# Cross-attention with image keys on one core: the statistics' transposes in another PSUM bank, and the result rows finished by ScalarE and GpSimd

## What is computed

```python
q = _split_heads(hidden_states @ w_q, HEADS)
k = _split_heads(text @ w_k, HEADS)
v = _split_heads(text @ w_v, HEADS)
out_text = _merge_heads(_sdpa(q, k, v))
mask_ip = _ip_mask(bbox, B, S, hidden_states.dtype)
k_ip = _split_heads(ip_h @ w_k_ip, HEADS)
v_ip = _split_heads(ip_h @ w_v_ip, HEADS)
out_ip = _merge_heads(_sdpa(q, k_ip, v_ip, mask=mask_ip))
out = out_text + out_ip
out = out @ w_out + b_out
out = out + residual
```

## Time and profile before

| | |
|---|---|
| device time, three runs | 1300.4, 1300.65 (median), 1303.57 us |
| the profiled execution | 1301.75 us; its span 1300.0 us |
| granted TensorE clock, mean | 0.979; 1.00 from 300 to 1250 us |
| busy | PE 91%, PEld 86%, DVE 80%, ACT 66%, POOL 59% |
| steps in which every part of the pipeline has work | b = 2 to 61, 60 periods from 294.9 to 1253.95 us |

### The profile page before, as it was taken

How to read it: one execution, slowest core, us unless ns; L and a number is a source line. 1 busy time by engine, 2 the same in 40 slices (tenths; PEclk the granted TensorE clock), 3 DMA queues, 4 the chain that set the end, 5 groups by cost and what they waited for, 6 DMA issues and landing times.

```text
span 1300.0 us, 34051 instructions
## 1 busy us (share of the span) xinstructions
PE 1179.9 (91%) x12734; PEld 1120.3 (86%) x12734; DVE 1040.8 (80%) x2182; ACT 857.4 (66%) x1795; POOL 760.8 (59%) x876
## 2 busy tenths in 40 slices
PE   6999878489999999999999999999999999999986
PEld 5898878379999998999999999999999999999885
DVE  5688865568888888888888888888888888888883
ACT  2343433467777777777777777777777777777772
POOL 0111110057777777777777777777777777777774
PEclk9999988789999999999999999999999999999998
DMA  6388887655455444454554444444545454555431
GB/s 168 66 190 176 155 155 145 109 108 119 111 114 114 111 111 113 110 118 113 114 111 111 111 111 111 111 111 111 116 115 116 115 116 114 116 111 113 101 73 41
DMA packets 361459, 151.30 MB, mean 116 GB/s; under 512 B 298641, under 2 KB 350865, under 8 KB 360017
## 3 DMA queue, kind: packets, MB, share of 16 engines
q1 hardware_dynamic: 361296, 149.13, 52.0%
HBM read 88.17 MB, written 39.90 MB: 99 GB/s over the span
## 4 chain that ended last, share of the span: by engine, by line
PE 56%; DVE 19%; ACT 9%; issue 6%; SPq 3%; POOL 2%; DMA 1%; DVEq 0%; POOLq 0%
PE ps_a L832 12%; PE ps_b L832 10%; PE ps_s L877 7%; PE ps_o L907 7%; PE ps_s L883 6%; PE ps_m L853 5%; DVE q_hi_lo L1271 4%; DVE heads L1303 4%; DVE aT_lo L1311 4%; ACT aT_hi L1053 3%; ACT prob L1068 3%; PE ps_v L199 3%; PE ps_a L818 2%; PE ps_k L199 2%; DVE inv L1299 2%
## 5 line engine op out<-in xcount | busy, mean ns | idle before, releaser
L1399 POOL TENSOR_TENSOR prob_lo<-prob,prob_hi 128x512 f16<-128x512 f32 (+1 forms) x448 | 486.6, 1099 | 228.5 <-ACT prob_hi L1069 228.3
L1068 ACT ACTIVATE prob<-ps_s 128x512 f32<-128x512 f32 (+1 forms) x448 | 253.3, 565 | 224.4 <-PE ps_s L883 223.9
L877 PE MATMUL ps_s<-q_hi_lo,keys 128*128 128x256 f32 x960 | 262.4, 310 | 6.2 <-DMA q_hi_extra<-q_hi_lo 6.1
L1069 ACT ACTIVATE prob_hi<-ps_s 128x512 f16<-128x512 f32 (+1 forms) x448 | 250.7, 560 | 0.0
L883 PE MATMUL ps_s<-q_hi_extra,keys 128*128 128x256 f32 x960 | 235.5, 282 | 0.0
L1289 DVE TENSOR_REDUCE stats<-ps_m 128x8 f32<-128x552 f32 x320 | 231.0, 722 | 0.0
L907 PE MATMUL ps_o<-values,prob_hi 128*128 128x68 f16 (+7 forms) x3584 | 199.5, 192 | 27.1 <-DVE heads L1303 27.1
L907 PEld LDWEIGHTS ps_o<-values,prob_hi 128*128 128x128 f16 x3584 | 175.3, 98 | 55.5 <-issue 41.1
L907 PE MATMUL ps_o<-values,prob_lo 128*128 128x68 f16 (+3 forms) x1792 | 190.3, 192 | 0.0
L877 PEld LDWEIGHTS ps_s<-q_hi_lo,keys 128*128 128x128 f32 x960 | 172.7, 190 | 6.6 <-DMA q_hi_extra<-q_hi_lo 6.5
L883 PEld LDWEIGHTS ps_s<-q_hi_extra,keys 128*128 128x128 f32 x960 | 173.7, 190 | 0.1
(11 more groups left out here) (179 smaller groups left out, 2916.6 us busy)
## 6 DMA issues: line engine op xcount, KB each, us to landing
x_in<-in_x_dram SPq DMA_DIRECT2D x64, 320.0 KB, 2.9
q_hi_extra<-q_hi_lo SPq DMA_DIRECT2D x64, 320.0 KB, 3.3
x_keep<-in_x_dram SPq DMA_DIRECT2D x64, 320.0 KB, 4.2
out_dram<-y SPq DMA_DIRECT2D x128, 160.0 KB, 2.9
k_scratch<-k_stage SPq DMA_DIRECT2D x16, 770.0 KB, 5.7
keys<-k_scratch SPq DMA_DIRECT2D x256, 48.1 KB, 2.1
ctx_in<-in_ctx_dram SPq DMA_DIRECT2D x64, 128.0 KB, 2.8
keys<-k_scratch SPq DMA_DIRECT2D x256, 24.1 KB, 1.9
```

Source lines behind the costliest of these rows:

```text
L877: mm(ps, keys[:, n, 0, quad, c:c + P], q_hl[n][:, quad, :], start=i == 0, stop=False)
L1068: nc.scalar.activation(prob[:, s, 0:w], ps_s[(b[1] + s) % 2][:, 0:w], ACT.Exp)
L1069: nc.scalar.activation(prob_hi[par(b)][:, s, 0:w], ps_s[(b[1] + s) % 2][:, 0:w], ACT.Exp).then_inc(s_hi, 1)
L1399: nc.gpsimd.tensor_tensor(prob_lo[par(b)][:, s, 0:w], prob[:, s, 0:w], prob_hi[par(b)][:, s, 0:w], ALU.subtract).then_inc(s_lo, 1)
```

## The change

Four things are done together.

1. `stats_transpose` writes into `ps_m`, the bank of the maxima, in place of `ps_b`, and stands behind the second piece of the query projection, ahead of the step's last `sum_heads`. The first `max_scores` of the next step now waits until ScalarE has copied the transposed statistics. ScalarE's copy of them moves ahead of `exps(6)`, and its spreading over the four other parts stands ahead of the last `q_hi`.
2. `a_hi` moves ahead of `exps(0)` on ScalarE.
3. `finish` is split: ScalarE copies the projected rows from PSUM into `y` (`y_out`, new, behind `exps(1)` and `exps(2)`), GpSimd adds `x_keep` in place (`finish`, both behind `rest(3)`). `x_transpose` and the drain's `attn_transpose` wait for ScalarE's copies (`s_ye`), the store still for the addition (`s_yr`).
4. On VectorE the three `spread_values` no longer stand in a row: one behind `maxima(0)`, one behind `maxima(2)`, one behind `image_maxima`; and `norm(1)` stands ahead of the second `q_lo`.

```diff
 # TensorE
-                            pe.wait_ge(s_yr, at(b, NT, -3 * NT))
+                            pe.wait_ge(s_ye, at(b, NT, -3 * NT))
                         else:
                             wait(pe, s_qlo, b, QUADS, 0)
-                            wait(pe, s_ex, b, 2, -2)
...
                     def max_scores(b, h4):
                         if h4 == 0:
                             pe.wait_ge(s_keys[third(b)], nth3(b, 16 * NKDMA))
+                            wait(pe, s_ex, b, 2, -1)
...
-                            last = nc.tensor.transpose(ps_b[:, t * P:(t + 1) * P], stats[:, t, :], ident[:])
+                            last = nc.tensor.transpose(ps_m[:, 0, t * P:(t + 1) * P], stats[:, t, :], ident[:])
...
-                    def attn_transpose(b, A, Bs):
-                        if Bs:
-                            pe.wait_ge(s_ex, at(b, 2, 5))
+                    def attn_transpose(b, A):
...
                             project(e, 1)
+                        if A:
+                            stats_transpose(a)
                         if Cs:
                             sum_heads(c, 3)
...
 # ScalarE
+                        def y_out(t):
+                            act.wait_ge(s_op, at(d, NT, t + 1))
+                            if t == 0 and (n is None or n >= 4):
+                                act.wait_ge(s_y[par(d)], nth(d, 32, -32))
+                            nc.scalar.copy(y[par(d)][:, t, :], (ps_a, ps_b)[t][:, 0:D]).then_inc(s_ye, 1)
...
 # VectorE
-                        def finish(t):
-                            dve.wait_ge(s_op, at(d, NT, t + 1))
...
-                            nc.vector.tensor_tensor(y[par(d)][:, t, :], (ps_a, ps_b)[t][:, 0:D], x_keep[par(d)][:, t, :],
-                                                    ALU.add).then_inc(s_yr, 1)
...
 # GpSimd
+                        def finish(t):
+                            pool.wait_ge(s_ye, at(d, NT, t + 1))
+                            if t == 0:
+                                pool.wait_ge(s_xb, at(d, 1, 1))
+                            nc.gpsimd.tensor_tensor(y[par(d)][:, t, :], y[par(d)][:, t, :], x_keep[par(d)][:, t, :],
+                                                    ALU.add).then_inc(s_yr, 1)
...
                         if Bs:
                             rest(3)
+                        if Ds:
+                            finish(0)
+                            finish(1)
+                        if Bs:
                             rest(4)
```

More of the change, by code:

```diff
@@ L567, in xattn_kernel @@
             s_yr = sem("y_ready")
+            s_ye = sem("y_evacuated")
             s_xk = [sem(f"residual_loaded{q}") for q in range(2)]
@@ L918, in attn_transpose @@
                         else:
-                            wait(pe, s_yr, b, NT, 0)
+                            wait(pe, s_ye, b, NT, 0)
                         for t in range(NT):
@@ L946, in step @@
                         if Ds:
-                            attn_transpose(d, A, Bs)
+                            attn_transpose(d, A)
                         if Bs:
@@ L1054, in a_hi, with extra_quads @@
                             nc.scalar.activation(aT2[0:64, :], ps_b[0:64, 0:S], ACT.Copy, scale=f[0:64]).then_inc(s_ahi, 1)
+                        def y_out(t):
[3 more added lines that the diff above has]
+                            nc.scalar.copy(y[par(d)][:, t, :], (ps_a, ps_b)[t][:, 0:D]).then_inc(s_ye, 1)
                         def extra():
                             act.wait_ge(s_et, at(a, 1, 1))
-                            nc.scalar.copy(q_ex[par(a)][QD:P, 0, :], ps_b[QD:P, 0:S]).then_inc(s_ex, 1)
+                            nc.scalar.copy(q_ex[par(a)][QD:P, 0, :], ps_m[QD:P, 0, 0:S]).then_inc(s_ex, 1)
+                        def extra_quads():
                             act.wait_ge(s_ex, at(a, 2, 1))
@@ L1074, in step @@
                                 tail_hi(1, u)
-                        if Bs:
-                            exps(0)
                         if Ds:
@@ L1079, in step @@
                         if Bs:
+                            exps(0)
                             exps(1)
+                        if Ds:
+                            y_out(0)
+                        if Bs:
                             exps(2)
+                        if Ds:
+                            y_out(1)
+                        if Bs:
                             exps(3)
@@ L1090, in step @@
                             q_hi(1)
+                        if A:
+                            extra()
                         if Bs:
                             exps(6)
+                        if A:
+                            extra_quads()
                         if E:
                             q_hi(2)
-                        if A:
-                            extra()
                     sched(act, step)
@@ L1352, in step @@
                             norm(0)
[L1353 to L1354 removed]
                         if A:
                             maxima(2)
[L1357 to L1358 removed]
+                        if Bs:
+                            spread_values(1)
                         if A:
@@ L1365, in step @@
                             image_maxima()
+                        if Bs:
+                            spread_values(2)
                         if E:
                             q_lo(0)
-                            q_lo(1)
                         if Cs:
@@ L1371, in step @@
                         if E:
+                            q_lo(1)
                             q_lo(2)
```

17 lines of the change are left out of this document (2 added, 15 removed).

## The result

The changed kernel takes **1320.15 us** (median of 4 runs, 1319.25 to 1321.02) against 1300.66 for the kernel before: ratio 1.0152, 95% interval 1.0138 to 1.0166. The forecast was 1321 us. Its profiled execution took 1320.81 us with a span of 1318.6 us, 18.6 more than the span before (1300.0).

What follows compares the result with a forecast made beforehand. After the change a ring through GpSimd was to bound the kernel: 15.73 + 0.50 = 16.23 us a step against 15.98. 1301.75 + 15.0 + 5.4 = 1322.1 profiled, less 1.1, gave 1321 us; range 1288 to 1345 held 0.86.

Steps and rivals of the forecast that it cites:

- The ring: rest(0), GpSimd's step to add_heads(1), PE transposes, a_hi, exps(0), next rest(0): 15.73 us free, 16.23 with collisions.
- The collisions: Spreadings on VectorE beside GpSimd: first free, large one behind maxima(2) 0.34, small one behind image_maxima 0.16, together 0.50 us.
- GpSimd rows of 1.2 to 1.5 us: Sign of collisions: GpSimd operations lengthened to this from 0.88 and 1.17 us.
- a wait of PE of 1 us or more: Sign: one new PE wait per step at the transposes, for GpSimd's attn, of this size.
- The additions to `y`: Two new GpSimd operations in its step, 0.83 us each, 1.66 in all, without waiting.
- The drain: Last steps become rings without mask, 16.08 us: +1.5 and +3.0; last rows pass GpSimd's 0.87: +0.9.
- SP: Stores wait for GpSimd until 10.9 us after a_hi; 3.2 of 5.3 us slack used, nothing late.
- no collision costs: Rival: VectorE's spreadings meet GpSimd without delaying it; ring 15.73 us, kernel 1290 us; chance 0.13.
- All three paid: Rival: the first spreading also delays GpSimd, +0.33 a step; ring 16.56 us, kernel 1341 us; chance 0.23.
- Whole blocking: Rival: two spreadings stop GpSimd for their whole length, 0.57 + 0.40; ring 16.70, kernel 1350 us; chance 0.10 (1350 and over).
- PE would be freed: Rival: the ring is not the bound, PE loses both waits, 46 us less; kernel 1255 us; chance 0.04.
- at nothing as long as PE is not early: Cost of max_scores' new wait for the statistics copy; the earlier norm was to gain at most 23.9 us.

Runs made afterwards that it cites:

- The run with one input: Changed kernel, each scattered spreading made a reduction over own_rows alone, one SBUF input and no product with the values: 1290.49 us.
- part 2 alone: Kernel before with one edit, a_hi ahead of exps(0) on ScalarE: 1274.57 us, ratio 0.9789.
- the second of these runs: Kernel before with statistics in the maxima's bank and the earlier norm, ScalarE's wide statistics copy put behind q_hi(2): 1342.4 us, ratio 1.0315.

## Why the prediction was right

**The ring.** It named the engine, the new wait and, within 0.05 us, the period. By `a_hi` at 295.66 and 1266.25 us, 60 steps are 16.18 us each, where it said 16.23 and before was 15.98. Its terms, from the rows above: `rest(0)` to the end of `add_heads(1)` 13.45 us, forecast 13.00 + 0.50; from there to `a_hi` (602.33 to 602.96) 0.63, forecast 0.64; from `a_hi` to `rest(0)` (602.96 to 605.04) 2.08, forecast 2.09.

**The collisions.** In a steady step they come in the places named and in size as said: none for the first spreading, 0.33 for the large one (said 0.34) and 0.15 for the small one (0.16). One sign that it gave, GpSimd rows of 1.2 to 1.5 us, does not show there: the delays fell on the short `attn` (0.65) and the `y` pair (1.86). Another, a wait of PE of 1 us or more, came out at 0.87. The run with one input, 15.69 us a step, shows both halves of the sum apart: 0.49 us of collision make the difference between 0.29 less than before and 0.20 more.

**The additions to `y`.** The undisturbed pair is 1.71 us as a row, and 1.67 to the next start; the sum took 1.66. (The line through the short and the long `attn` gives 1.54 at 640 columns, a little over the 1.52 of the earlier trace rows, and not "as seen".)

**How the 18.6 us come together.** 60 x 0.193 = 11.6 in the steady steps, where 15.0 was said. The drain's `a_hi` stand here:

```profile
1266.25 0.69 ACT L1047 ACTIVATE aT_hi<-ps_a,value_scale 128x512 fp32r<-128x512 f32 x1 [2.24 <-PE ps_b L919]
1282.57 0.69 ACT L1047 ACTIVATE aT_hi<-ps_a,value_scale 128x512 fp32r<-128x512 f32 x1 [4.37 <-PE ps_b L919]
1298.87 0.69 ACT L1047 ACTIVATE aT_hi<-ps_a,value_scale 128x512 fp32r<-128x512 f32 x1 [7.33 <-PE ps_b L919]
```

Two steps of 16.32 and 16.30 us where the earlier trace rows have 14.57 and 13.04: 1.8 and 3.3 (said 1.5 and 3.0, since a step without mask was taken as 16.08). Two things were left out there. In the first step a third spreading, from 1277.40 to 1278.07, meets three `rest`, which take 3.23 us and not 2.92:

```profile
1277.60 3.23 POOL L1403 TENSOR_TENSOR prob_lo<-prob,prob_hi 128x512 f16<-128x512 f32 x3
```

In the second, the stretch from the end of `add_heads(1)` (1297.87) to `a_hi` is 1.00 us and not 0.64. PE had stood idle for 4.4 us before it, TensorE's granted clock is 0.50 there, 1.2 GHz, against 1.00 until 1294 us, and the first two transposes take 0.69 us and not 0.44.

What follows is 19.7 against 18.4 (1300.0 - 1281.56): 1.3, said 0.9. In all 6.3 and not 5.4. The first steps, which the sum held at nothing, gave +0.75 (295.66 against 294.91). So 11.6 + 6.3 + 0.75 = 18.6. The largest miss is the period: said 0.25 longer than before, measured 0.19, which is 3.4 us in 60 steps. Drain (0.9) and start (0.75) gave back half of that. Half of what was left came from outside the span: 2.2 us of device time lie around it, 1.75 before, and the median stands 0.7 below the profiled execution and not 1.1, together 0.9 more than the forecast had. That the total hit within 1 us is therefore in part luck.

**SP.** The stores began at 613.41, 10.45 us after `a_hi`, when the first addition was done. Both additions were done at 614.37, 11.4 us after it, where the prediction has 10.9: that figure left out its own 0.50 of collisions. Nothing behind the stores was late: no compute engine's list of steady waits names a transfer.

**The rivals.** None of them came. That no collision costs is the one that a run could build: with one input it is 1290.5 us, and the prediction said 1290. All three paid would have needed the short `attn` at 618.17 or at 602.00 lengthened too; it is 0.32 and 0.33. Whole blocking would have cost 0.97 a step, measured 0.49. That PE would be freed (1255 us) was held against GpSimd's sum; even part 2 alone, where the ring has slack, stops at 1274.57.

**What it did not see.** It put part 1 "at nothing as long as PE is not early" and credited it up to 23.9 us. In the changed kernel the ring hides it, so the forecast held, but the runs show part 1 as a loss elsewhere: 54.8 us alone, and 22 on top of part 2, 16 of them from one copy's place on ScalarE. It also gave VectorE's side of the collisions no term. In the changed kernel that was right, but the scattered spreadings alone cost 50.5 us in a kernel where GpSimd bounds nothing, by longer rows on VectorE, by their place, or both.

## What to carry to other kernels

An engine that is 59% busy and bounds nothing can become the bound with few added microseconds, if an edit elsewhere makes its first operation wait for what its last one released. Follow the waits round the step, add the durations, and compare with the period before moving anything. And test parts of a change one by one: here one exchanged pair of calls was worth 26 us (2.1%), the rest took more than that away.

## What the runs showed of the hardware

The size of part 1's loss was not expected. GpSimd's operations and VectorE's products of two SBUF inputs delay each other: GpSimd lost 0.33 us to a spreading of 0.57 and 0.15 to one of 0.40, while VectorE lost 0.25 us on the large one (0.82 and not 0.57) and 0.7 on the small one (1.09 and not 0.40). Three spreadings in a row beside one `rest` took 2.34 us and not 1.37, while the `rest` took 1.25 to 1.53 and not 1.17: the larger share can fall on either engine, and which one stands before the bound decides what it costs. In the second of these runs the small spreading of the row starts inside the `rest` (608.50 to 610.03), at 608.93, and ends at 610.30. That is 1.37 us, of which 1.10 lie inside the `rest`; undisturbed it is 0.40 us long. So it may have stood until the `rest` was nearly done, though no row shows the wait itself. Why the same meeting costs `rest(0)` 0.08 us in one run and 0.36 in the other was not settled.
